# Two LoRA layers with a gated mixture: where the adapters' rows are staged, when T3 is split, and how the logits are computed

## The reference

```
def cond(x, W, bias, A, B, scale, id):            # A, B: the adapter of each batch entry
    return x @ W.T + bias + scale[id] * ((x @ A[id].T) @ B[id].T)

def ffn(x, Wb, bb, Wr, LA, LB):                   # 8 experts of rank 16
    probs = softmax(x @ Wr.T)
    p, i = top_k(probs, 2);  p = p / sum(p)
    w = sum(one_hot(i, 8) * p[..., None], axis=1)
    h = einsum('td,erd->ter', x, LA)
    return x @ Wb.T + bb + 2.0 * einsum('ter,eor,te->to', h, LB, w)

x = x + ffn0(cond0(x));   x = x + ffn1(cond1(x))
```

## Time and profile before

| | us |
|---|---|
| median of 3 runs | 695.09 (694.82 to 696.44) |
| the profiled execution | 697.44 |
| its span | 695.8 |
| TensorE busy | 685.2 (98%) |
| VectorE busy | 417.5 (60%) |
| GpSimd busy | 261.9 (38%) |
| ScalarE busy | 229.5 (33%) |
| DMA | 147.22 MB, mean 212 GB/s |

### The profile page before, as it was taken

How to read it: one execution, slowest core, us unless ns; L and a number is a source line. 1 busy time by engine, 2 the same in 40 slices (tenths; PEclk the granted TensorE clock), 3 DMA queues, 4 the chain that set the end, 5 groups by cost and what they waited for, 6 DMA issues and landing times.

```text
span 695.8 us, 9234 instructions
## 1 busy us (share of the span) xinstructions
PE 685.2 (98%) x3341; PEld 604.4 (87%) x3341; DVE 417.5 (60%) x671; ACT 229.5 (33%) x407; POOL 261.9 (38%) x219
## 2 busy tenths in 40 slices
PE   8999999999999999999999999999999999999997
PEld 7999999877888888888899999998778888888886
DVE  6564677669735476652573753795897236846423
ACT  6334335644212044220504244254542302422200
POOL 2472113045673150493124322030738524207820
PEclk9999999999999999999999999999999999999999
DMA  8245857993678936357832744789836986545633
GB/s 330 73 148 184 271 186 224 387 355 117 229 246 289 308 106 204 90 157 242 310 126 77 252 152 172 242 305 356 306 106 227 299 308 200 162 141 151 203 100 121
DMA packets 74210, 147.22 MB, mean 212 GB/s; under 512 B 7412, under 2 KB 38260, under 8 KB 74166
## 3 DMA queue, kind: packets, MB, share of 16 engines
q1 hardware_dynamic: 70614, 138.12, 59.2%
q10 hardware_dynamic: 2016, 6.42, 2.8%
q0 software_dynamic: 1536, 2.10, 1.0%
HBM read 98.42 MB, written 47.32 MB: 209 GB/s over the span
## 4 chain that ended last, share of the span: by engine, by line
PE 79%; DMA 8%; DVE 8%; SPq 2%; ACT 1%; issue 1%; ACTq 0%
PE ps L466 25%; PE ps L468 25%; PE ps L467 25%; DMA form_scratch<-f_hl 5%; DVE x_hl L940 5%; DMA bwr_scratch<-bwr 3%; PE ps L541 2%; PE ps L595 2%; DMA e_raw<-in_ext 1%; DVE x_raw L1132 1%; PE ps L567 1%; SPq L346 1%; SPq L353 1%; DVE hg_hl L940 0%; PE ps L577 0%
## 5 line engine op out<-in xcount | busy, mean ns | idle before, releaser
L466 PE MATMUL ps<-x_hl,a_hl 128*128 128x512 f32 x448 | 175.9, 393 | 3.1 <-ACT u L850 3.1
L468 PE MATMUL ps<-x_hl,a_hl 128*128 128x512 f32 x448 | 174.5, 390 | 0.0
L467 PE MATMUL ps<-x_hl,a_hl 128*128 128x512 f32 x448 | 174.4, 389 | 0.0
L466 PE MATMUL ps<-e_hl,w_hl 128*128 128x400 f32 (+1 forms) x432 | 146.2, 339 | 1.0 <-DVE e_hl L940 0.7
L468 PE MATMUL ps<-e_hl,w_hl 128*128 128x400 f32 (+1 forms) x432 | 146.0, 338 | 0.0
L467 PE MATMUL ps<-e_hl,w_hl 128*128 128x400 f32 (+1 forms) x432 | 145.9, 338 | 0.0
L466 PEld LDWEIGHTS ps<-x_hl,a_hl 128*128 128x128 f32 x448 | 84.1, 188 | 20.6 <-ACT u L850 3.6
L468 PEld LDWEIGHTS ps<-x_hl,a_hl 128*128 128x128 f32 x448 | 84.1, 188 | 17.7
L467 PEld LDWEIGHTS ps<-x_hl,a_hl 128*128 128x128 f32 x448 | 84.1, 188 | 17.2
L466 PEld LDWEIGHTS ps<-e_hl,w_hl 128*128 128x128 f32 x432 | 81.2, 188 | 2.8 <-DVE w_hl L940 2.0
L467 PEld LDWEIGHTS ps<-e_hl,w_hl 128*128 128x128 f32 x432 | 81.1, 188 | 0.0
(11 more groups left out here) (118 smaller groups left out, 978.2 us busy)
## 6 DMA issues: line engine op xcount, KB each, us to landing
a_hl<-form_scratch SPq DMA_DIRECT2D x112, 512.0 KB, 4.3
form_scratch<-f_hl SPq DMA_DIRECT2D x56, 512.0 KB, 7.1
e_raw<-in_ext SPq DMA_DIRECT2D x12, 580.0 KB, 8.2
w_raw<-in_w ACTq DMA_DIRECT2D x12, 512.0 KB, 3.4
x_raw<-in_xT SPq DMA_DIRECT2D x6, 1024.0 KB, 6.7
x_raw<-x_scratch SPq DMA_DIRECT2D x6, 1024.0 KB, 8.3
x_scratch<-x_raw SPq DMA_DIRECT2D x16, 256.0 KB, 3.2
out_T<-x_raw SPq DMA_DIRECT2D x16, 256.0 KB, 2.8
```

Source lines behind the costliest of these rows:

```text
L466: nc.tensor.matmul(dst, w_hi, m_hi, start=start, stop=False, skip_group_check=again)
L467: nc.tensor.matmul(dst, w_hi, m_lo, start=False, stop=False, skip_group_check=again)
L468: return nc.tensor.matmul(dst, w_lo, m_hi, start=False, stop=stop, skip_group_check=again)
```

## The change

- `bw_st` moves from the keep area into the slot of B22 in `x_hl`, which is free until B22 is split. So `keep_w1` in s = 0 waits for `form_lo`, `form_sum` and `px_lo` of the last-but-one pair instead (what lay in `p_raw` under `u2`), GpSimd's `make_t3` no longer waits for the staged rows, and ScalarE's split of B22 in s = 0 waits for `d_bw`, `stack_out` and `d_stack[1]`. ScalarE writes `bw_st` only once all fold units are done.
- `stack` and `bw_st` rows become `EXT` wide and take the router columns with them; `bwr`, `rlog`, `bwr_scratch` and their DMAs go.
- `px_hl` holds only the experts' columns, in rows of 128 floats; the router's eight go to `pr_hl` (one more copy and one more subtraction per fold row). Router columns are copied three times into `s_hl`, with 16 zero columns between, so that the S bank has router rows at 64, 80 and 112.
- The logits become matmuls in float32r of 128 rows with the operands of `low_mv` and `stack`: rows 96 to 127 of `low_mv` hold the router results' high and low part, which `low_rest` (VectorE, new) makes out of ScalarE's rounded copy `sx_r` and the S bank, against an identity in `stack`. The bias is added in `routing` from `bias_r`.
- VectorE's order: in the second chunk `adapters` comes behind two of the four outputs of C11, then the other two, `low_rest`, T1, `routing`, T1, and only then the split of T3. `s_split` for the next pair comes behind `gated`. ScalarE's order: `keep_w5(g, 0)` ahead of `hg_split(g, 1)`.

```diff
+RPARTS = 2 * NE
 RHI = 2 * LOW
-SROWS = RHI + 2 * NE
+SROWS = RHI + RPARTS
+RZERO = SROWS + RPARTS
+RAGAIN = RZERO + RPARTS
...
+        bw_st = place("bw_st", [P, 2, EXT], f32r, slot_at + SLOT_OF[0][B22] * KH * 2 * CH * 4)
...
-        bw_st = place("bw_st", [P, 2, EXT], f32r, keep_at)
-        px_hl = place("px_hl", [P, KT, 2, HX_PITCH], f32r)
-        stack = [place(f"stack{i}", [P, D + ER], f32r) for i in range(2)]
+        px_hl = place("px_hl", [P, KT, 2, ER], f32r)
+        pr_hl = place("pr_hl", [P, KT, 2, NE], f32r)
+        stack = [place(f"stack{i}", [P, EXT], f32r) for i in range(2)]
...
-                sp.dma_start(rlog[tb][0:LOW, :], bwr[rows, :]).then_inc(d_stack[tb], 16)
...
-                sp.dma_start(rlog[tb][0:LOW, :], bwr_dram[l, rows, :]).then_inc(d_stack[tb], 16)
...
-                sp.dma_start(bw_dram[l], bw_st[2 * LOW:P, :, 0:D + ER].bitcast(f32)).then_inc(S["d_bw"], 16)
-                sp.dma_start(bwr_dram[l], bwr[2 * LOW:P, :]).then_inc(S["d_bw"], 16)
+                sp.dma_start(bw_dram[l], bw_st[2 * LOW:P, :, :].bitcast(f32)).then_inc(S["d_bw"], 16)
...
-                pe.wait_ge(S["sxr_done"], u + 1)
                 for t in range(TT):
-                    last = nc.tensor.matmul(ps[:, S_BANK, t * NE:(t + 1) * NE], sx[:, t * P:(t + 1) * P],
-                                            rlog[tb][:], start=True, stop=True)
+                    last = nc.tensor.matmul(ps[:, S_BANK, t * NE:(t + 1) * NE], low_mv[tb][:, t * P:(t + 1) * P],
+                                            stack[tb][:, D + ER:EXT], start=True, stop=True)
...
-                nc.scalar.copy(px_hl[:, k_of(r), 0, 0:HX], p_raw[:, pair % 2, half, D:EXT]).then_inc(S["px_hi"], 1)
+                nc.scalar.copy(px_hl[:, k_of(r), 0, :], p_raw[:, pair % 2, half, D:D + ER]).then_inc(S["px_hi"], 1)
+                nc.scalar.copy(pr_hl[:, k_of(r), 0, :], p_raw[:, pair % 2, half, D + ER:EXT]).then_inc(S["px_hi"], 1)
...
+                elif block == B22:
+
+                    act.wait_ge(S["d_bw"], 16 * (l + 1))
+                    act.wait_ge(S["stack_out"], l + 1)
+                    act.wait_ge(d_stack[1], 48 * (g + 1))
...
-                nc.scalar.copy(sx[RHI:SROWS, :], ps[RHI:SROWS, S_BANK, :]).then_inc(S["sxr_done"], 1)
+                if u:
+                    act.wait_ge(S["low_r"], u)
+                nc.scalar.copy(sx_r[RZERO:P, :], ps[RHI:RZERO, S_BANK, :]).then_inc(S["sxr_done"], 1)
...
                 if g % SUPER == 0:
-                    act.wait_ge(S["d_bw"], 32 * (l + 1))
-                    act.wait_ge(S["stack_out"], l + 1)
-                    act.wait_ge(d_stack[1], 64 * (g + 1))
+
+                    act.wait_ge(S["form_lo"], NM * (KH * l + KH - 1))
+                    act.wait_ge(S["form_sum"], len(SUMS) * (KH * l + KH - 1))
+                    act.wait_ge(S["px_lo"], 2 * (KT * l + KT - 2))
...
+                    keep_w5(g, 0)
                     hg_split(g, 1)
-                    for m in range(2):
-                        keep_w5(g, m)
+                    keep_w5(g, 1)
...
+            def low_rest(g, tb):
+                u = 2 * g + tb
+                dve.wait_ge(S["sxr_done"], u + 1)
+                if g:
+                    dve.wait_ge(S["pe_out"], 16 * (g - 1) + (12, 16)[tb])
+
+                nc.vector.scalar_tensor_tensor(low_mv[tb][STACK:P, :], sx_r[STACK:P, :].bitcast(f32), sign_sb[STACK:P, :],
+                                               ps[STACK:P, S_BANK, :], op0=ALU.mult, op1=ALU.add
+                                               ).then_inc(S["low_r"], 1)
                 dve.wait_ge(S["low_hi"], u + 1)
                 sub(low_mv[tb][2 * LOW:STACK, :], sx[0:LOW, :],
                     low_mv[tb][0:LOW, :].bitcast(f32)).then_inc(S["low_lo"], 1)
-                if more:
-                    s_split(l, c + 1)
...
-                    for m in range(KH):
-                        out_c11(g, m)
-                    sum_split(g, T3, w57)
-                    adapters(l, g, 1, more)
+                    out_c11(g, 0)
+                    out_c11(g, 1)
+                    adapters(l, g, 1)
+                    out_c11(g, 2)
+                    out_c11(g, 3)
+                    low_rest(g, 1)
                     made_split(g, T1, range(2))
                     routing(g, 1)
                     made_split(g, T1, range(2, 4))
+                    sum_split(g, T3, w57)
                     for m in range(KH):
                         keep_u2(g, m)
                     gated(g, 1)
+                    if more:
+                        s_split(l, 2 * s + 2)
```

More of the change, by code:

```diff
@@ L19 @@
 EXT = D + ER + NE
-HX = ER + NE
 NOB = -(-EXT // 512)
@@ L179, in fused_layers @@
         low_b = place("low_b", [LOW, CH], f32)
-        sx = place("sx", [SROWS, CH], f32)
+        sx_at = at[0]
+        sx = place("sx", [P, CH], f32)
+        sx_r = place("sx_r", [P, CH], f32r, sx_at)
         low_mv = [place(f"low_mv{i}", [P, CH], f32r) for i in range(2)]
@@ L187, in fused_layers @@
         mul_sb = place("mul_sb", [2 * LOW, BATCH], f32)
-        rlog = [place(f"rlog{i}", [SROWS, NE], f32) for i in range(2)]
-        bwr = place("bwr", [P, NE], f32)
+        sign_sb = place("sign_sb", [P, 1], f32)
+        eye_sb = place("eye_sb", [P, NE], f32)
+        halves_sb = place("halves_sb", [P, BPC], f32)
+        bias_r = place("bias_r", [P, NE], f32)
         bias_sb = place("bias_sb", [P, KT + 1], f32)
@@ L819, in first_stack @@
                     act.wait_ge(S["pe_out"], 16 * SUPER * l)
-                nc.scalar.copy(rlog[0][0:LOW, :], bwr[0:LOW, :])
-                for cols, done in ((slice(D, D + ER), "stack_in"), (slice(0, D), "stack_out")):
+                for cols, done in ((slice(D, EXT), "stack_in"), (slice(0, D), "stack_out")):
                     for i, hl in enumerate((0, 1, 0)):
@@ L1200, in _ @@
                         last.then_inc(S["mul_done"], 1)
-                dve.wait_ge(S["px_lo"], KT * (l + 1))
-                nc.vector.tensor_copy(s_hl[:, :, RHI:SROWS].rearrange("p k (h e) -> p k h e", h=2),
-                                      px_hl[:, :, :, ER:HX]).then_inc(S["router_cols"], 1)
+                        if l == 0:
+                            sub(sign_sb[STACK:P, :], halves_sb[STACK:P, 0:1], halves_sb[STACK:P, 1:2])
+                            for tb in range(2):
+                                nc.vector.tensor_copy(stack[tb][STACK:P, D + ER:EXT], eye_sb[STACK:P, :]
+                                                      ).then_inc(S["eye_done"], 1)
+                dve.wait_ge(S["px_lo"], 2 * KT * (l + 1))
+                for o in (RHI, SROWS, RAGAIN):
+                    nc.vector.tensor_copy(s_hl[:, :, o:o + RPARTS].rearrange("p k (h e) -> p k h e", h=2),
+                                          pr_hl[:]).then_inc(S["router_cols"], 1)
                 g = SUPER * l
@@ L1369, in _ @@
                     pool.wait_ge(S["acc_zero"], 1)
-                    for i, pad in enumerate((stack[0][STACK:P, :], stack[1][STACK:P, :],
-                                             low_mv[0][STACK:P, :], low_mv[1][STACK:P, :],
-                                             s_hl[:, :, SROWS:P])):
+                    for i, pad in enumerate((stack[0][STACK:P, 0:D + ER], stack[1][STACK:P, 0:D + ER],
+                                             s_hl[:, :, RZERO:RAGAIN])):
                         if i:
```

85 lines of the change are left out of this document (37 added, 48 removed).

## The result

The changed kernel takes 691.72 us (median of six, 691.28 to 693.44); the kernel before, beside it, 695.77 us (median of six, 694.64 to 697.22). The ratio is 0.9943, 95% interval 0.9927 to 0.9958: 4.0 us faster (2.9 to 5.1), where 7.1 were forecast and the range ended at 691.0. The two profiled executions took 697.44 and 691.28 us, 6.2 us apart.

What follows compares the result with a forecast made beforehand. TensorE's stream of matmuls bounds the kernel (busy 685.2 of 695.8 us). Terms -3.6 + 1.8 - 1.7 - 3.2 - 0.4 = -7.1 us took the 695.09 us median to 688.0 us, range 684.9 to 691.0.

Steps and rivals of the forecast that it cites:

- The rest: nothing: Extra copies and subtractions per fold row, further small copies, fewer pads: none on TensorE, priced at nothing, bounds 0 and +0.5.
- the stop for `u`: TensorE's waits for ScalarE's W1 copy (line 850) before W2, once per layer: 1.97 + 1.64 = 3.61 us.
- Staging in B22's slot: W1's copy no longer waits for staged rows' readers, so both stops before W2 go: -3.61 us; B22's split waits nothing.
- rival C: B22's split waits for the scratch copies, stopping second-chunk routers about 3 us per layer; 694.5 us, chance 0.05.
- What is late next: New stop before W2's third product, on ring place 6's load: 0.9 us per layer, +1.8 us; bounds +2.7 and +0.7.
- rival A: The ring isn't late: the queue gains more without the 32-byte rows, no new W2 stop; 686.2 us, chance 0.27.
- Adapters ahead of T3's split: VectorE's second chunk in s = 0: low part ready 3.1 us earlier, near 170.4, low-row stop goes: -1.7 us.
- T3 and the order of keeps: T3's later split delays `hg`'s low part in s = 1 by 2.48 of 5.3 us to spare; priced at nothing.
- Logits: Four instructions instead of eight per group, at 101 ns each: 0.41 us saved in each of 8 groups, -3.2 us.
- Rows of 512 bytes: 24 matmuls with experts' folded weights take 5.46 us instead of 5.51, by row pitch: -0.4 us, bounds 0 and -0.4.
- Rival D: T3's late split meets GpSimd and lasts 6.9 us, stopping TensorE before experts' rows of every pair; 699 us, chance 0.04.
- Rival B: Half the gain: ring stop +2.7, low-row -0.8, logits -1.6, pitch -0.2, sum -3.5; 691.6 us, chance 0.19.

Runs made afterwards that it cites:

- after_again: One of two unchanged copies of the changed kernel, profiled again; the copies measured 691.25 us and a median of 692.26 us (ratio 0.9944).
- aligned: The changed kernel with every tile of 512 bytes or more placed at a multiple of 128 bytes; 689.61 us (0.9896), copy on another chip 689.99 us (0.9914).
- t3_early: The changed kernel with VectorE's old order in the second chunk: four outputs, T3's split, then adapters; 693.04 us, ratio 0.9956.
- best: The aligned kernel with the load of ring place 6 issued ahead of the load of B22 in s = 0; 689.65 us, ratio 0.9898.
- bw_last2: The aligned kernel with SyncE issuing ring place 5, B22, place 6 and then the store of the staged rows; 689.14 us, ratio 0.9900.
- before_shifted: The kernel before with 64 bytes left free ahead of stack0, moving `stack` and the tiles behind it; 697.73 us, ratio 1.0011.

## Why the prediction was wrong

Two steps failed. "The rest: nothing" left out products that got slower by 2.4 us in all, most of it by the places of the tiles, and the stop for `u` was taken at the length that one profiled execution showed, the longest of four. The waits that were to go and the one that was to come are as forecast.

**Staging in B22's slot.** The stops at line 850 are gone in every profile, by the mechanism named, and B22 isn't held: its load landed at 147.64, 1.8 us earlier than in the earlier trace rows, and GpSimd started with it. So rival C is out for this kernel: the staged rows' store landed at 143.6, ahead of B22. The term "-3.6" failed in size. It was the longest of what are now four profiles (1.4 to 3.6, mean 2.6), because the stop ends with a DMA whose landing varies. I took it for a constant, and then took the 2.35 us by which that execution lay above its median for something that both kernels would have: 1.0 us of it was this very stop (3.6 - 2.6), counted as a gain and not given back.

**What is late next.** Forecast +1.8, found +1.4 in the mean of eight profiles (0.9 in the three of after itself). The load of place 6 was issued at 135.9 and landed at 148.9, where it was 139.9 and 150.6 before: 4 us earlier out, 1.7 us earlier in. That is the row of the kernel after, with its time from issue to landing:

```profile
L357 SPq DMA_DIRECT2D a_hl<-form_scratch x1: 711/711/711, 135.9 to 135.9; - x1
DMA to landing us min/median/max: 13.0/13.0/13.0
```

In after_again and aligned it landed at 150.4 and 150.8, so even this gain isn't there each time: the queue sets the landing, as argued. The forecast counted on the small rows for the hole in the earlier trace rows. Two such DMAs went from ahead of this load (not three, as I wrote), and the hole stayed. All DMAs of the kernel after from 136 to 146 us, in 40 slices:

```profile
GB/s 393 385 426 410 467 377 423 355 318 214 230 158 276 290 282 340 398 316 439 412 342 496 308 365 419 386 439 336 442 401 401 401 393 385 393 393 385 410 401 410
```

Over these ten us the mean is 370, 340 and 361 GB/s in the three profiles of after and 347, 353, 340 and 362 in the four of before. By the rule of the Trainium skill that stood behind rival A (DMA: Bandwidth & Descriptors, Specifications), the short rows were the trouble; they went, and neither the hole nor, in most profiles, the stop went with them. The three stack copies out of 32 partitions are still in that stretch. No run took either away alone, so what makes the hole is open.

**Adapters ahead of T3's split.** Forecast -1.7, found -1.7, and shown by t3_early. The low part was ready at 167.7 rather than 170.4, because VectorE came to this chunk 2.4 us earlier (161.66 against 164.06). I hadn't followed B22's landing, which sets this: in layer 0 the first output of C11 starts 14.5 or 14.6 us behind the start of GpSimd's sum, which waits for B22's landing, in all five profiles of the old staging, and 13.9 to 14.0 us behind it in all twelve of the new one, from a landing at 147.6 (after) to one at 151.9 (best, where the stop is back). The way leads over GpSimd's sums T3 and T2: even in bw_last2, where ScalarE's split of B22 waits for the staged rows until 151.8, VectorE is no later.

**T3 and the order of keeps.** No cost, as forecast, with 2.5 us left where 5.3 - 2.5 = 2.8 were expected. Rival D is out.

**Logits.** Forecast 0.41 us a group and -3.2; found 0.81 - 0.36 = 0.45 and -3.6 over eight groups. The 101 ns of the forecast were a mean over a group whose first instruction takes only 28 ns; the four that went were of the 112 ns of the others, and 112 ns is the spacing of the new form too. By the Trainium skill (TensorE: Matmul & The Clock Gate, LDWEIGHTS) a load would set an estimated 107 ns, whatever its rows; the trace's 112 ns, the same for 80 rows and for 128, lie some 5 ns above it.

**Rows of 512 bytes.** Forecast -0.4, found 44.12 to 43.73 us over the eight groups, -0.4. The match is in part luck: in aligned they take 43.52 us, -0.6, and the other 0.2 us is what the slower router group ahead of each leaves behind. It is likely the same effect of the weights' place as in the next paragraph (rows of 576 bytes start in turns on and 64 bytes off a multiple of 128). The forecast priced it here and not for the tiles that the change moved.

**"The rest: nothing; bounds 0 and +0.5."** This step failed. I counted added instructions and found none on TensorE, but didn't ask where the tiles come to lie. The router products cost 29.87 us against 29.07 (+0.80), the products with `stack` and the experts 60.11 against 59.17 (+0.94), and of the seven products all that no stop touches 279.80 against 279.15 (+0.65): +2.4 us. Of these aligned gives back 0.80, 0.60 and 0.33, about 1.7, and 1.7 to 2.6 in the medians. The last +0.65 does not appear in before_shifted (279.16), so it isn't shown to come from the places alone; where the half that aligned leaves comes from is open. (Two pads went and not three, which changes nothing.)

The terms now read -2.6 + 1.4 - 1.7 - 3.6 - 0.4 + 2.4 = -4.5 us, against 4.0 measured (2.9 to 5.1); with the ring's 0.9 us of the three profiles of after alone they would be -5.0, still within the interval. For the two profiled executions they close as well: -3.6 + 0.7 - 1.7 - 3.6 - 0.4 + 2.4 = -6.2, and 6.2 us lie between them. From the forecast to the time, 688.0 to 691.72: +1.0 for the stop taken at its longest, +2.4 for the slower products, -0.4 for the logits, -0.4 for the ring, and +0.7 because the kernel before itself came out at 695.77 and not 695.09: 3.3 of 3.7 us. Rival B had the sum right (691.6) by luck, its reasons are wrong: the low-row stop went whole, the logits gave more and not less, the ring's stop was smaller than the forecast's and not larger, and the pitch gave all of its 0.4 us.

## What to carry to other kernels

A stop that ends with a DMA is no constant: read it in several executions before it is made a term of a sum, and keep its spread in the range. Whoever changes a tile's size moves all tiles behind it, so compare the time per matmul of the groups that weren't touched; rounding places to 128 bytes was worth more here (1.7 to 2.6 us in the medians) than any of the three other orders of the queue, none of which is told from aligned. A mean over a short group hides that its first instruction costs less: take the spacing inside it. When a stop is taken away, say who is late next, and follow the loader as well as the reader.

## What the runs showed of the hardware

- Sixteen float32r matmuls of 512 columns took 3.63 us with their weights' tile at 128 past a multiple of 256 bytes in a partition, 3.67 at 64 and 3.73 or 3.74 at 192, without a wait and with the data's tile where it was.
- A float32r matmul with 128 columns and rows of weights and 8 columns of data started 112 ns behind the last; the fp32 form of 80 rows cost two instructions of 112 ns. The second of a group followed the first after 26 to 28 ns.
- A load issued 4 us earlier into a full queue landed 1.7 us earlier in one execution. Issued 3.4 us earlier in another it landed 0.2 us earlier, and issued 2.6 us earlier in a third (137.3 against 139.9) 0.2 us later (150.8 against 150.6). One kernel's stops that end with a DMA lay between 1.4 and 3.6 us in four executions.
- The queue's rate fell to between 158 and 340 GB/s for about 2 us in the kernel without the 32-byte rows too.
